# Conv-and-attention block on one NeuronCore: order of norm, third pooling level and low parts at the seam of two images

## The chip, the cores and the metric

The kernel runs on one core of a Trainium2 chip. The metric is the device time of one execution in microseconds; lower is better. All times in this text are microseconds unless marked ns. Engines: TensorE (PE in the profile; PEld is its weight load), VectorE (DVE), ScalarE (ACT), GpSimd (POOL), SyncE (SP).

## The reference

The input x is (8, 256, 32, 32), float32. Two blocks are applied, each on a group-normalised input and added to its own input:

```python
x = x + L0(_gn(x), ...)     # pooling and gated convolution
x = x + L1(_gn(x), w1, w2)  # attention over the 1024 pixels of an image

def L0(x):
    x_aux = silu(conv1x1(x, w_sta) + b)             # 256 -> 128 channels
    y1, y2 = [x_aux], [x_aux]
    for _ in range(3):
        y1.append(0.9 * maxpool5x5(y1[-1]) + 0.1 * sumpool5x5(y1[-1]) / 25)
        y2.append(sumpool5x5(e * y2[-1]) / (sumpool5x5(e) + 1e-6))   # e = exp(y - max)
    y = concat([silu(cv1(concat(y1))), silu(cv2(concat(y2)))])       # 512 channels
    a = y, through four depthwise convolutions of 3 taps (1x3, 3x1, dilated 1x3, dilated 3x1)
    a = conv1x1(a, w_c1)
    return silu(cvend(y * a))

def L1(x):   # per image, f: 1024 x 256
    q = f @ w1.T;  attn = softmax(q @ f.T / 16);  v = f @ w2.T
    return attn @ v
```

`_gn` normalises each image over groups of 8 channels: mean and variance over 8 channels and all pixels.

## The kernel before

All products are made of float32 matmuls whose operands are split in a high and a low part (each tile has a `_hi` and a `_lo`): three matmuls, hi x hi, lo x hi and hi x lo, stand for one. ScalarE makes the high parts (a copy), VectorE the low ones (value minus high part).

Phases A and B (up to about 270) normalise the input, make x_aux of all images, and the y2 levels of all images in HBM. Phase C is a loop over images, written as `step(i, conv, attn, chained, ahead)` on every engine, with an order of its own per engine, written out by hand. Step i does the convolution part of image i (`conv`), the attention part of image i - 1 (`attn`), and the pooling chain of image i + 1 (`chained`). Step 0 has no attention, steps 1 to 7 are full steps (both parts; in step 7 nothing is chained), step 8 has the attention of image 7 alone. Engines meet by counting semaphores.

TensorE in a full step: cv2(0), cv2(1) with a small matmul for the group means inside, then one for the group variances, cv1(0), cv1(1), q and v of the attention, then eight tiles of scores, transposes and products with v, then c1 (four) and cvend (two). A `product_split` of the convolution is 12 uses of a weight tile, each two matmuls of 512 columns. cv1(0) takes the low part of level 1 at use 7, that of level 2 at use 8, the high part of level 3 at use 9 and its low part at use 11. PSUM has three slots that rotate: product n can start when the reader of product n - 3 is done. The slot of the first v product (`("qv", 2)`) is that of the fourth cv product, which ScalarE's `silu_cv(3)` frees.

The pooling chain of an image: three levels (`middle` twice, `last`), each 5x5 maxima by VectorE (`maxima`, steps 0 to 6, the last one on `work_b`), 5x5 sums by accumulating DMAs that POOL issues one after another (`add_round`, eight rounds a level), and a mixture of both by VectorE (`mixture_of_added`, a wait on `columns_added`). `level_split_hi` and `level_split_lo` make the parts of a level for cv1. POOL's queue at a step's seam: last round of level 3, wait for its landing, the two first DMA issues of the next image's level 1 (L226, L228), the power for the norm (L1195), and then the accumulations of that level.

The norm of the attention input (image i - 1): VectorE `bn_stats` and `bn_aggr` at the end of step i - 1, TensorE `means` over channel groups, VectorE three small operations (dev, its square, spread), TensorE `variances`, VectorE two small operations (eps, negated mean), POOL the power -0.5, VectorE `shift`; ScalarE then makes the normalised image and its high part in two tiles, VectorE the low parts (`normalised_lo`), which q's product wants behind its first four matmuls.

The depthwise taps: ScalarE does the centre tap of a piece (`centre_tap(n)`), VectorE the two outer ones (`outer_taps(n)`); a centre tap waits for the outer taps of the piece's stage before.

## Time and profile before

| | us |
|---|---|
| median of three runs | 1384.13 |
| lowest, highest | 1377.48, 1387.42 |
| the profiled execution | 1376.88 |
| its span, first to last instruction | 1375.1 |
| busy in the span: TensorE, VectorE, ScalarE, POOL | 1206.2, 1152.7, 726.0, 293.6 |
| mean granted TensorE clock | 0.96 of full |

The profile is that of one execution. Around its span lie 1.8. Busy time of matmuls is modelled, as they are pipelined. In a timeline row, what stands in brackets is the idle time of the engine before that row and what ended it. A transfer's row is its issue alone.

### The profile page before, as it was taken

The page shows a single profiled execution, that of the slowest core. Times are in us where ns is not written, and L with a number is a line of the kernel's source. Part 1 is how long each engine was busy: PE and PEld are TensorE (multiplying, and loading weights), DVE is VectorE, ACT ScalarE, POOL GpSimd, SP SyncE. Part 2 cuts the span into 40 slices and gives each one's busy share as a digit, 9 for nine tenths or more (in the row PEclk, how much of TensorE's full clock was granted, in tenths as well). Part 3 has the DMA queues.
Part 4 walks back from the last instruction along what each step waited for, and adds up shares of the span by engine and source line. Part 5 has one row for each costly group of instructions (what it writes and reads, how often), then busy time and mean ns, then how long its engine had stood idle before and what let it go on. Part 6 is the DMA issues. An engine that isn't in the chain of part 4 may idle for free.

```text
span 1375.1 us, 17821 instructions
## 1 busy us (share of the span) xinstructions
PE 1206.2 (88%) x6730; PEld 1026.1 (75%) x6730; DVE 1152.7 (84%) x1220; ACT 726.0 (53%) x781; POOL 293.6 (21%) x247
## 2 busy tenths in 40 slices
PE   3559898766899999999899999999998999999697
PEld 1249898655678877877788788878887887797597
DVE  7779887799989889989998999899989977985343
ACT  0246667663375447536753675366546643853342
POOL 1566767401111111111111111111111111000000
PEclk9769999987999999999999999999999999999899
DMA  7403123253665566566456644764475466001000
GB/s 287 168 31 93 77 86 115 97 126 90 142 143 118 151 177 122 113 169 160 107 121 197 141 109 108 208 140 104 116 200 126 108 144 157 0 1 62 0 0 31
DMA packets 72303, 159.91 MB, mean 116 GB/s; under 512 B 33088, under 2 KB 35904, under 8 KB 72256
## 3 DMA queue, kind: packets, MB, share of 16 engines
q0 software_dynamic: 23904, 92.11, 29.9%
q1 hardware_dynamic: 47648, 66.85, 14.7%
q8 instruction: 32, 0.52, 0.2%
q10 hardware_dynamic: 704, 0.30, 0.1%
q14 instruction: 15, 0.12, 0.0%
HBM read 41.46 MB, written 25.17 MB: 48 GB/s over the span
## 4 chain that ended last, share of the span: by engine, by line
PE 36%; DVE 18%; issue 17%; ACT 6%; DMA 3%; DVEq 0%; POOL 0%; ACTq 0%; POOLq 0%
PE slot L1299 12%; PE slot L1246 10%; PE ps_level L1299 10%; DVE between L1574 4%; PE slot L1315 3%; DVE a L1574 2%; DMA boxes<-twos 2%; DVE pt_all L345 1%; ACT a L1478 1%; ACT between L1428 1%; DVE f_all L410 1%; DVE x L1617 1%; ACT f_all L1447 1%; ACT a L1428 1%; DVE tall L323 1%
## 5 line engine op out<-in xcount | busy, mean ns | idle before, releaser
L1299 PE MATMUL ps_level<-v_all,pt_all 128*128 128x256 f32 x1536 | 200.1, 287 | 13.6 <-DVE pt_all L1578 8.2
L1299 PEld LDWEIGHTS ps_level<-v_all,pt_all 128*128 128x128 f32 x1536 | 189.6, 192 | 17.3 <-DVE pt_all L1578 15.8
L1299 PE MATMUL slot<-f_all,q_all 128*128 128x512 f32 x768 | 189.7, 397 | 0.0
L1574 DVE SCALAR_TENSOR_TENSOR a<-between,k_columns,a 128x992 f32<-128x992 f32 (+1 forms) x128 | 157.6, 1232 | 6.9 <-ACT a L1428 4.6
L1299 PEld LDWEIGHTS slot<-f_all,q_all 128*128 128x128 f32 x768 | 140.1, 188 | 27.9
L1578 DVE TENSOR_TENSOR pt_all<-slot,pt_all 128x1024 fp32r<-128x1024 f32 x64 | 78.2, 1221 | 40.8 <-ACT pt_all L1442 40.6
L1451 ACT CAST v_all<-y 128x1024 fp32r<-128x1024 f32 x32 | 33.8, 1055 | 134.6 <-DVE y L1607 134.4
L1456 ACT ACTIVATE mixed<-ps_level,row_inv 128x256 f32<-128x256 f32 x64 | 30.2, 473 | 133.5 <-PE ps_level L1299 133.5
L1428 ACT ACTIVATE a<-between,k_columns 128x1024 f32<-128x1024 f32 x64 | 79.3, 1240 | 33.3 <-DVE between L1574 32.3
L1607 DVE SCALAR_TENSOR_TENSOR y<-slot,k_columns,y 128x1024 f32<-128x1024 f32 x32 | 40.9, 1282 | 57.0 <-PE slot L1246 55.1
L1574 DVE SCALAR_TENSOR_TENSOR between<-y,k_columns,between 128x992 f32<-128x992 f32 x64 | 78.8, 1249 | 7.8 <-ACT between L1428 6.6
L1442 ACT CAST pt_all<-slot 128x1024 fp32r<-128x1024 f32 x64 | 65.1, 1017 | 36.2 <-PE slot L1315 35.3
L1583 DVE TENSOR_REDUCE c_minus_max<-slot 128x1 f32<-128x1024 f32 x64 | 78.0, 1219 | 7.0 <-PE slot L1299 7.0
L1437 ACT ACTIVATE pooled<-slot,c_minus_max 128x1024 f32<-128x1024 f32 x64 | 71.6, 1118 | 21.8 <-DVE c_minus_max L1583 21.8
L1315 PE MATMUL slot<-k_ident,pooled 128*128 128x128 f32 x512 | 67.2, 274 | 15.9 <-ACT pooled L1437 15.9
L1574 DVE SCALAR_TENSOR_TENSOR between<-a,k_columns,between 128x960 f32<-128x960 f32 x64 | 77.2, 1215 | 1.1
L1315 PEld LDWEIGHTS slot<-k_ident,pooled 128*128 128x128 f32 x512 | 56.8, 141 | 19.9 <-ACT pooled L1437 19.9
L873 POOL TENSOR_TENSOR e_lo<-x_all,e_hi 128x1024 fp32r<-128x1024 f32 x24 | 61.3, 2552 | 43.4 <-ACT e_hi L828 43.4
L1246 PE MATMUL slot<-f_all,k_c_hi 128*128 128x512 f32 x232 | 64.7, 401 | 0.4 <-DVE y L1607 0.4
L1246 PE MATMUL slot<-f_all,k_c_lo 128*128 128x512 f32 x232 | 63.5, 396 | 0.0
L1246 PE MATMUL slot<-q_all,k_c_hi 128*128 128x512 f32 x232 | 63.5, 395 | 0.0
L1246 PE MATMUL slot<-q_all,k_cv_hi 128*128 128x512 f32 x192 | 59.4, 412 | 2.2 <-ACT q_all L405 2.2
(204 smaller groups left out, 2752.1 us busy)
## 6 DMA issues: line engine op xcount, KB each, us to landing
levels<-x_all SPq DMA_DIRECT2D x32, 512.0 KB, 2.6
boxes<-twos POOLq DMA_DIRECT2D x28, 543.0 KB, 4.8
boxes<-twos POOLq DMA_DIRECT2D x28, 527.0 KB, 4.6
x_all<-in_x SPq DMA_DIRECT2D x8, 1024.0 KB, 12.8
f_all<-levels SPq DMA_DIRECT2D x8, 1024.0 KB, 7.4
x<-in_x SPq DMA_DIRECT2D x8, 1024.0 KB, 5.9
out<-x SPq DMA_DIRECT2D x8, 1024.0 KB, 4.1
twos<-boxes POOLq DMA_DIRECT2D x14, 561.0 KB, 3.0
```

Of the source, the lines that this page charges most:

```text
L873: nc.gpsimd.tensor_tensor(e_lo[:, u], e[u], e_hi[:, u].bitcast(F32), ALU.subtract).then_inc(e_lo_done, 1)
L1246: last = nc.tensor.matmul(slot[:, hs], weights[:, k], inputs(k)[:, hs], start=(at == 0), stop=(at == len(uses) - 1))
L1299: last = nc.tensor.matmul(out, lhs, rhs, start=(n == 0), stop=(n == len(parts) - 1))
L1315: last = nc.tensor.transpose(slot[:, cols(m)], prob[:, cols(m)], keep["ident"][:, :])
L1428: nc.scalar.activation(dst, src, ACT.Identity, scale=keep["taps"][:, s, c, 1:2], bias=keep["b_taps"][:, s, c:c + 1]).then_inc(taps_centre. ...
L1437: nc.scalar.activation(prob[:, :], slots_of["s", t][:, :], ACT.Exp, bias=minus_max[:, t:t + 1], accum_out=row_sum[:, t:t + 1]).then_inc(pr ...
L1442: nc.scalar.copy(pt_hi[:, t % 2], slots_of["t", t][:, :]).then_inc(pt_hi_done.sem, 1)
L1451: nc.scalar.copy(y_hi[:, m], y[:, m]).then_inc(y_hi_done.sem, 1)
L1574: nc.vector.scalar_tensor_tensor(o, u, keep["taps"][:, s, c, tap:tap + 1], o, ALU.mult, ALU.add).then_inc(taps.sem, 1)
L1578: nc.vector.tensor_tensor(pt_lo[:, t % 2], slots_of["t", t][:, :], pt_hi[:, t % 2].bitcast(F32), ALU.subtract).then_inc(pt_lo_done.sem, 1)
L1583: nc.vector.tensor_reduce(minus_max[:, t:t + 1], slots_of["s", t][:, :], AX, ALU.max, negate=True).then_inc(maxed.sem, 1)
L1607: nc.vector.scalar_tensor_tensor(y[:, m], slots_of["c1", m][:, :], keep["b_c1"][:, m:m + 1], y[:, m], ALU.add, ALU.mult).then_inc(gated.se ...
```

## The change

It concerns the seam between two steps. On VectorE the three small operations of the norm come right behind maximum step 5 of level 3's maxima (step 6 follows them), eps and negated mean behind that; the third mixture then, low part 1 behind it, shift, low parts 2 and 3. Before, the order was maxima 5 and 6, low parts 1 and 2, small operations, mixture, eps and negated mean, low part 3, shift. The two low parts of the normalised image stand together, with both tap pairs behind them. At the end of step 0 the maxima 3 to 6 of level 3 leave their place between the sums of the two halves of the image and go behind the aggregation. On TensorE the variances' matmul goes from behind cv2(1) to behind its use 9. On ScalarE `silu_cv(1)` and the high part of level 3 change places.

```diff
@@ -1229,7 +1229,7 @@
                 def cols(m):
                     return slice(m * P, (m + 1) * P)
 
-                def product_split(kind, m, name, hi, lo, sig, order, hi_ready, lo_ready, between=None):
+                def product_split(kind, m, name, hi, lo, sig, order, hi_ready, lo_ready, between={}):
 
 
                     slot = claim(kind, m)
@@ -1245,8 +1245,8 @@
                             hs = slice(h * HALF, (h + 1) * HALF)
                             last = nc.tensor.matmul(slot[:, hs], weights[:, k], inputs(k)[:, hs],
                                                     start=(at == 0), stop=(at == len(uses) - 1))
-                        if between and at == len(uses) // 2:
-                            between()
+                        if at in between:
+                            between[at]()
                     last.then_inc(sig.sem, 1)
 
                 def tiles_of(t):
@@ -1255,7 +1255,7 @@
                 def when(sig):
                     return lambda n: wait(pe, sig, i, n + 1)
 
-                def cv2(m, between=None):
+                def cv2(m, between={}):
                     product_split("cv", m, "cv2", pooled.hi, pooled.lo, cv, pooled.ORDER, when(pooled.hi_done),
                                   when(pooled.lo_done), between)
 
@@ -1359,10 +1359,9 @@
                     cv2(0)
                     if not attn:
                         box_first()
-                    cv2(1, between=means if attn else None)
+                    cv2(1, between={6: means, 9: variances} if attn else {})
                 elif attn:
                     means()
-                if attn:
                     variances()
                 if conv:
                     cv1(0)
@@ -1468,8 +1467,8 @@
                             inputs_hi(c - 1)
                 elif conv:
                     silu_cv(0)
+                    silu_cv(1)
                     chain.level_split_hi(act, i, LEVELS)
-                    silu_cv(1)
                     for n in range(CT):
                         centre_tap(n)
                 if attn:
@@ -1632,8 +1631,6 @@
 
                 slots_of = slot_plan(conv, attn)
                 before = iter(range(BEFORE if attn else KT * STAGES))
-                if conv and attn:
-                    chain.level_split_lo(dve, i, LEVELS - 1)
                 if attn:
                     small = Steps(dve, norm, i - 1)
                     wait(dve, group_mean, i - 1, 1)
@@ -1645,7 +1642,7 @@
                 if chained and not attn:
                     chain.maxima(dve, i + 1, 0, first=chain.inner_ahead())
                 if conv and attn:
-                    chain.mixture_of_added(dve, i, LEVELS - 1)
+                    chain.maxima(dve, i, LEVELS - 1, MIX - 2)
                 elif conv:
                     outer_taps(next(before))
                     chain.mixture_of_first(dve, image2d(ps_level[:, :]))
@@ -1654,10 +1651,14 @@
                     small.did(nc.vector.tensor_scalar(spread[:, :], ps_ot[:, 0:CT], 1e-5, None, ALU.add))
                     small.did(nc.vector.tensor_scalar(gmean[:, :], ps_o[:, 0:CT], -1.0, None, ALU.mult))
                     if conv:
-                        chain.level_split_lo(dve, i, LEVELS)
+                        chain.mixture_of_added(dve, i, LEVELS - 1)
+                        chain.level_split_lo(dve, i, 1)
                     small.wait()
                     wait(dve, rstd_done, i - 1, 1)
                     small.did(nc.vector.tensor_tensor(shift[:, :], gmean[:, :], rstd[:, :], ALU.mult))
+                    if conv:
+                        chain.level_split_lo(dve, i, LEVELS - 1)
+                        chain.level_split_lo(dve, i, LEVELS)
                 if conv:
                     outer_taps(next(before))
                 if conv and attn:
@@ -1665,7 +1666,8 @@
                 if attn:
                     for t in range(CT):
                         normalised_lo(t)
-                        if conv:
+                    if conv:
+                        for t in range(CT):
                             outer_taps(next(before))
                 if conv:
                     for n in before:
@@ -1739,7 +1741,6 @@
                     wait(dve, chain.first_max, i + 2, MIX - 1)
                     level_maxima(2, 0, 1, 2)
                     add_l0(0)
-                    level_maxima(2, 3, 4, 5, 6)
                 else:
                     if ahead:
                         ahead_maxima(0, 1, 2)
@@ -1780,9 +1781,9 @@
                     for m in range(CT):
                         nc.vector.bn_aggr(mv[:, m, :], stats[:, m].rearrange("p h s -> p (h s)")).then_inc(bn.sem, 1)
                 if chained:
-                    if attn:
-                        level_maxima(2, 5, 6)
-                    chain.level_split_lo(dve, i + 1, 1)
+                    if not attn:
+                        level_maxima(2, 3, 4)
+                    level_maxima(2, 5)
 
             for n in range(KT):
                 pooled.split_lo(dve, 0, n)
```

## Rows read from the trace of the kernel before

**Rows 1.** Windows from one step's means to the next; x: instructions.

```profile
core 0: us, PE busy (x) PEld busy (x) DVE busy (x) ACT busy (x) POOL busy (x), PEclk, DMA share, GB/s
...
507.35:638.33 130.98, 123.05 (x686) 104.87 (x685) 119.86 (x128) 73.37 (x81) 19.89 (x26) 1.00 0.60 143
638.33:769.93 131.60, 124.23 (x685) 105.99 (x684) 119.94 (x128) 73.60 (x81) 19.93 (x26) 0.99 0.59 141
```

**Rows 2.** TensorE's timeline: start us, us, what, [idle before it, releaser].

```profile
850.45 1.09 PE L1315 MATMUL slot<-k_ident,pooled 128*128 128x128 f32 x8 [1.99 <-ACT pooled L1437]
...
900.92 0.28 PE L1335 MATMUL ps_level<-c_mv,k_group 128*128 128x2 f32 x2
...
904.67 0.38 PE L1335 MATMUL ps_level<-c_spread,k_group 128*128 128x2 f32 x2 [1.03 <-DVE c_spread L1644]
...
919.61 1.27 PE L1299 MATMUL slot<-f_all,k_w_hi 128*128 128x512 f32 x4 [2.33 <-DVE f_all L1603]
...
931.52 5.62 PE L1299 MATMUL slot<-f_all,q_all 128*128 128x512 f32 x24
...
948.93 3.14 PE L1299 MATMUL ps_level<-v_all,pt_all 128*128 128x256 f32 x24 [1.36 <-DVE pt_all L1578]
```

**Rows 3.** VectorE's timeline of step 5.

```profile
899.26 0.28 DVE L1781 BATCH_NORM_AGGREGATE c_mv<-c_stats 128x2 f32<-128x12 f32 x2 [0.16 <-DVE c_stats L1620]
899.46 1.17 DVE L323 TENSOR_TENSOR work_b<-work_a 128x1024 f32<-128x1024 f32 x1
...
904.66 1.22 DVE L332 SCALAR_TENSOR_TENSOR last<-boxes,work_b 128x1024 f32<-128x1024 f32 x1
...
907.00 1.23 DVE L345 TENSOR_TENSOR pt_all<-last,v_all 128x1024 fp32r<-128x1024 f32 x1 [0.85 <-ACT v_all L341]
...
909.14 4.99 DVE L1574 SCALAR_TENSOR_TENSOR between<-y,k_columns,between 128x992 f32<-128x992 f32 x4 [0.85 <-ACT between L1428]
...
915.88 2.54 DVE L1574 SCALAR_TENSOR_TENSOR a<-between,k_columns,a 128x992 f32<-128x992 f32 x2 [0.61 <-ACT a L1428]
...
921.92 4.85 DVE L1574 SCALAR_TENSOR_TENSOR between<-a,k_columns,between 128x960 f32<-128x960 f32 x4
...
926.69 2.35 DVE L1690 SCALAR_TENSOR_TENSOR q_all<-slot,q_all 128x1024 fp32r<-128x1024 f32 x2
...
932.77 1.23 DVE L1693 TENSOR_TENSOR v_all<-slot,v_all 128x1024 fp32r<-128x1024 f32 x1 [0.22 <-ACT v_all L1496]
...
934.46 1.23 DVE L1583 TENSOR_REDUCE c_minus_max<-slot 128x1 f32<-128x1024 f32 x1 [0.47 <-PE slot L1299]
```

**Rows 4.** VectorE's timeline of step 8, the first small operation.

```profile
1289.66 0.16 DVE L1640 TENSOR_TENSOR c_dev<-c_mv,ps_level 128x2 f32<-128x2 f32 x1 [0.60 <-PE ps_level L1335]
```

**Rows 5.** ScalarE's timeline of step 5.

```profile
905.92 1.05 ACT L341 CAST v_all<-last 128x1024 fp32r<-128x1024 f32 x1 [6.94 <-DVE last L332]
...
923.19 1.10 ACT L1421 ACTIVATE y<-slot,k_columns 128x1024 f32<-128x1024 f32 x1
```

**Rows 6.** POOL's timeline of step 2 and of step 5.

```profile
509.68 0.56 POOL L226 DMA_DIRECT2D twos<-ahead  x1 [4.82 <-issue]
...
902.38 0.56 POOL L226 DMA_DIRECT2D twos<-ahead  x1 [4.71 <-DMA boxes<-twos]
...
906.16 0.71 POOL L1195 TENSOR_TENSOR c_rstd<-c_spread,k_minus_half 128x2 f32<-128x2 f32 x1 [2.69 <-DVE gmean L1655]
```

**Rows 7.** Windows of 5 us behind two TensorE waits, columns as in rows 1.

```profile
657.00:662.00 5.00, 4.99 (x15) 3.96 (x16) 4.93 (x5) 2.51 (x4) 0.43 (x1) 0.66 0.58 111
...
850.00:855.00 5.00, 3.97 (x32) 3.77 (x32) 4.96 (x7) 3.82 (x7) 0.00 (x0) 1.00 0.68 172
```

**Rows 8.** The mixture's line in phase B: durations in ns, first and last start.

```profile
L332 DVE SCALAR_TENSOR_TENSOR last<-last,work_b x1: 3223/3223/3223, 226.2 to 226.2; 128x1024 f32<-128x1024 f32 x1
```

**Rows 9.** The timeline of step 1, TensorE and VectorE.

```profile
375.49 0.58 PE L1335 MATMUL ps_level<-c_mv,k_group 128*128 128x2 f32 x2 [5.99 <-DVE c_mv L1781]
...
380.12 1.23 DVE L332 SCALAR_TENSOR_TENSOR last<-boxes,work_b 128x1024 f32<-128x1024 f32 x1 [2.00 <-DMA boxes<-twos]
```

## The prediction

> **What bounds the kernel now.** First the windows cut at the matmul of the group means, one per full step [rows 1]: a step takes 131 us, TensorE is busy for 123 to 124 and VectorE for 120 of them, so neither hides the other, and what ends last has to be read place by place. Steps 2 to 7 of the seven full steps (images 1 to 7) repeat one pattern; step 5, from 900.92, is the one I follow. TensorE's timeline there [rows 2] shows three waits in front of the attention loop: 1.03 for c_spread, 2.33 for the second low part of the normalised image, 1.36 for a low part of the turned probabilities. The first two look like the change's prize. VectorE's timeline [rows 3] is to be read second: from the aggregation at 899.26 to the row maximum at 934.46 it idles in small pieces only: 0.85 (low part of level 3, for ScalarE's cast), 0.85 (first tap, ScalarE), 0.61 (third tap pair, ScalarE), and 0.47 before the maximum. At the maximum it waits for TensorE, but soon after TensorE waits 1.36 for VectorE [rows 2]. So VectorE's order bounds this stretch, TensorE's two waits are mostly slack, and the gain is what VectorE gains at the row maximum. Behind 948.93 the pattern is rigid, with both engines in step; an advance there is carried to the next aggregation.
>
> **Part by part, steps 2 to 7, in the clock of step 5.** A use of two 512-column matmuls is 0.47 (24 matmuls in 5.62, [rows 2]); large VectorE operations start 1.14 apart where nothing holds them (two take 2.35) and 1.25 where one needs the other's result (a full 1.22 and a little) [rows 3].
>
> *Small operations and variances moved forward.* The aggregation and maximum step 5 stay, until 900.63. The first small operation needs the means (900.92); in step 8, with nothing beside it, VectorE gets them 0.60 after its aggregation, matmul included [rows 4], so it starts at about 901.45, a new idle of 0.8. Three small operations end at 902.0. TensorE's place for the variances, behind use 9, comes at 900.92 + 0.14 + 3 x 0.47 = 902.46: no wait, and the second product ends at 903.8 instead of 903.6; the first product of cv1 starts at 903.8 instead of 904.9. Maximum step 6 fills VectorE from 901.97, eps and gmean follow at 903.15.
>
> *Third mixture, low parts.* The mixture runs at 903.3 (before: 904.66), low part 1 at 904.56, shift at 905.75, low parts 2 and 3 at 905.85 and 907.0. Before, ScalarE's cast had waited 6.94 for the mixture with everything queued behind it [rows 5]. Now silu_cv(1) (1.1) stands in front of the cast and runs from 904.0, the cast runs 904.9 to 905.9, and the two centre taps end before VectorE wants them: both pieces of 0.85 go. The power on POOL (0.71, [rows 6]) ends by 904.2; it queues behind the next image's two DMA issues, to 903.5, and POOL's next accumulation comes no later than before. TensorE wants low part 1 at use 7 (907.1), 2 at use 8 (907.5), 3 at use 11 (908.9); they end at 905.8, 907.0, 908.2. No wait, margins 0.5 and more. VectorE's first tap: 908.1 instead of 909.14, gain 1.0.
>
> *Both normalised low parts together.* ScalarE runs 2.0 ahead of its old times, so they run at 913.0 and 914.2 and end at 915.4; TensorE wants them at 903.8 + 24 x 0.47 + 0.9 = 916.0. The 2.33 goes. The 0.61 before the third tap pair goes too (its centre tap had been waiting behind nothing but ScalarE's queue): tap pair 4 starts at 920.2 instead of 921.92, the q low part at 925.0 instead of 926.69, gain 1.7.
>
> *What is late next.* TensorE finishes q at 920.6 and needs a slot that silu_cv(3) frees. That stands on ScalarE behind centre tap 5, and that behind VectorE's tap pair 3, which ends at 920.3: silu_cv(3) ends at 922.5 (before: 923.19 + 1.10 [rows 5]). So a new wait of 1.9, then 0.7 for the q low part. The first scores end at 931.8, just when VectorE is free (925.0 + 2.3 for q's low parts, 2.4 for a tap pair, 2.3 for v's low parts, whose 0.22 wait before the second goes [rows 3]): the row maximum at 932.0. Against 934.46 that is 2.4. Step 5 is one of three slow steps, though: its 2.33 wait was followed by a granted clock of 0.66 of full, the 1.2 GHz level for part of it; such a step is 131.60 long against 130.98 [rows 1, 7]. Against the steps at full clock the gain is 1.8.
>
> *Clock.* Sum without slow steps: 3 x 2.4 + 3 x 1.8 = 12.6. After the wait of 1.99 at the end of the attention loop the windows show 1.00 [rows 2, 7], and my new wait is 1.9, so I count one slow step in six. Its price: a clock of 0.66 over 5 us loses 1.7 of matmul time, of which the 0.7 and a little more lie under the wait for the q low part, which then falls away: about 0.9 is left. So 12.6 - 0.9 = 11.7; at worst six times 0.9 = 5.4 off.
> By the Trainium skill (TensorE: Matmul & The Clock Gate, What's actually happening) the gate is released by activity and the throttled state is the default, its monitor running free of the kernel's start; by that, fewer and shorter waits can only help on average, but which step is hit is chance, as the alternation of slow and full steps here suggests.
>
> *POOL beside VectorE.* Before, every power ran while VectorE idled or had just started a small tail (906.16, beside the 0.85 idle [rows 3, 6]); now it runs beside the mixture. The nearest row is far: the mixture that ran beside 1024-element POOL work took 3.22 against 1.22 [rows 3, 8]. For 2 elements I take 0; the other end is the power's whole 0.7 per step, 4.2 in all.
> The Trainium skill speaks against the change here (GPSIMD Engine Reference, Specifications): GpSimd shares its SBUF interfaces with VectorE and contends with VectorE instructions that have two SBUF inputs, as the mixture has; the trace agrees for large operands [rows 8], and by that rule the sum would be 8 instead of 12.
>
> *Step 1.* The two last-image sums come earlier there, since four maximum operations move behind them: TensorE's 5.99 wait for the aggregation [rows 9] shrinks to 1.2, but a wait of 2.7 for the spread and 3.3 for low part 1 follow, because the column sums land only at 380.1, where VectorE waits 2.00 already. From that mixture on, VectorE has 1.25 + 1.14 + 0.1 + 2 x 1.14 = 4.8 to its first tap instead of 4.48 (as in step 5, 904.66 to 909.14, idle included), and saves the 0.6: gain 0.3. Step 8 is not changed. In all 11.7 + 0.3 = **12.0 us**.
>
> **The rivals.**
> (A) *The column sums become the wait.* The mixture is wanted 1.4 earlier, at means + 2.4. POOL saw the sums at means + 1.46 in step 5 and + 2.33 in step 2 [rows 1, 2, 6]: margins 0.9 and 0.1. Where they land 1.5 or more later, each step does what step 1 does, 0.3: 7 x 0.3 = 2.1, 1382. For: step 1, thin margins, medians 7 above the profiled run. Against: the profile's own times. Chance 0.15.
> (B) *TensorE was the bound.* Then both waits count in full, and the slow clock of three steps: 6 x (1.03 + 2.33) + 3 x 0.6 = 22, 1362. Against: VectorE's queue, as above. Chance 0.09.
> (C) *Contention with POOL in full*: 12.0 - 4.2 = 8, 1376. Chance 0.12.
> (D) *Slower: late sums plus the clock.* If sums land later than means + 5 (use 7 of cv1's first product is passed by then), TensorE stops inside that product and again for silu_cv(3), runs at 1.2 GHz into the scores, and loses the 1.7 of row 7 against 0.3 gained: 6 x 1.4 = 8 slower, 1392. Place: level_lo_done in cv1(0). Chance 0.04.
> (E) *The variances stall the product anyway*, if the spread comes after 902.46 (margin 0.5). That is TensorE's slack and costs nothing until it exceeds what VectorE bounds; inside the forecast.
>
> **How the numbers follow.** The profiled execution took 1376.88 (span 1375.1), at the low end of the three runs (1377.48 to 1387.42); its rows give 1376.88 - 12.0 = 1364.9. On the median, 1384.13 - 12.0 = **1372**, 0.9% less. Chance 0.60 for this case, own range 1366 to 1377 (no slow step: 12.9 less; all slow: 7.5 less). The range 1362 to 1383 reaches to (C), (A) and (B), and takes in some 3 us of either median. One per cent, about what a measurement of this kernel can tell from no change, is 1370.3: below it lie (B) and some four tenths of the forecast, 0.35; above 1398 only the tail of (D), 0.03.
>
> **What would show it.** Right: no wait for c_spread inside the product, variances about 1.5 after the means; low parts of the normalised image back to back with no TensorE wait; a new TensorE wait near 1.9 for y (silu_cv(3)) before v's product; the row maximum 32.7 behind the aggregation (now 35.2); steps of 129 us. Wrong: VectorE idle at the mixture for columns (A), a mixture over 1.3 us (C), the first tap pair not earlier than aggregation + 9.5, or a full-step period that shrinks by 3 or more (B).

## The result and the profile after

The changed kernel takes 1368.84 (median of 8 runs, 1363.71 to 1373.67) against 1382.41 of the kernel before (8 runs, 1377.33 to 1387.45). The ratio is 0.9897, 95% interval 0.9871 to 0.9923: 1.0% faster, 14 us. Forecast: 1372, 0.9% and 12 us. The profiled execution took 1367.99, its span is 1366.2.

The windows cut at the group means again, steps 2 to 5 (these answer to [rows 1]):

```profile
core 0: us, PE busy (x) PEld busy (x) DVE busy (x) ACT busy (x) POOL busy (x), PEclk, DMA share, GB/s
...
509.07:638.06 128.99, 122.72 (x686) 104.99 (x685) 119.56 (x127) 73.46 (x81) 20.93 (x26) 1.00 0.60 144
638.06:768.56 130.50, 124.23 (x686) 106.54 (x684) 119.63 (x127) 73.27 (x81) 20.66 (x26) 0.99 0.57 139
768.56:901.11 132.55, 125.82 (x685) 107.92 (x684) 119.92 (x127) 73.42 (x81) 20.38 (x26) 0.97 0.59 141
901.11:1031.12 130.01, 123.00 (x685) 104.93 (x684) 119.75 (x127) 73.48 (x81) 20.43 (x26) 1.00 0.61 145
```

Steps of 129.0, 130.5, 132.6 and 130.0 stand where there were 131.0 and 131.6. They are not alike any more, and two things make them differ: late column sums and the granted clock. VectorE's timeline of step 5 shows the first, as [rows 3]. The aggregation is its row L1782, the row maximum its first row L1582 (the first maximum over a tile of scores):

```profile
899.44 0.28 DVE L1782 BATCH_NORM_AGGREGATE c_mv<-c_stats 128x2 f32<-128x12 f32 x2 [0.16 <-DVE c_stats L1619]
...
901.43 0.16 DVE L1637 TENSOR_TENSOR c_dev<-c_mv,ps_level 128x2 f32<-128x2 f32 x1 [0.62 <-PE ps_level L1335]
...
903.45 1.23 DVE L332 SCALAR_TENSOR_TENSOR last<-boxes,work_b 128x1024 f32<-128x1024 f32 x1 [0.17 <-DMA boxes<-twos]
...
906.71 0.16 DVE L1658 TENSOR_TENSOR c_shift<-gmean,c_rstd 128x2 f32<-128x2 f32 x1 [0.68 <-POOL c_rstd L1195]
...
909.10 4.99 DVE L1573 SCALAR_TENSOR_TENSOR between<-y,k_columns,between 128x992 f32<-128x992 f32 x4
914.00 2.35 DVE L1602 TENSOR_TENSOR f_all<-a,f_all 128x1024 fp32r<-128x1024 f32 x2
...
921.17 4.85 DVE L1573 SCALAR_TENSOR_TENSOR between<-a,k_columns,between 128x960 f32<-128x960 f32 x4
925.94 2.35 DVE L1692 SCALAR_TENSOR_TENSOR q_all<-slot,q_all 128x1024 fp32r<-128x1024 f32 x2
...
933.09 1.22 DVE L1582 TENSOR_REDUCE c_minus_max<-slot 128x1 f32<-128x1024 f32 x1 [0.16 <-PE slot L1299]
```

The three idle pieces of ScalarE's making (0.85, 0.85, 0.61) are gone; from the shift on VectorE doesn't wait until the row maximum. In their place stand 0.62 for the means, 0.17 for the column sums and 0.68 for the power. The first tap starts 9.66 behind the aggregation, little earlier than the 9.88 of before; in step 2, where sums and power were in time, it is 8.67. The row maximum comes 33.65 behind the aggregation here, 32.66 in step 2; before it was 34.6 or 35.2.

TensorE in step 5, as [rows 2]:

```profile
901.11 0.28 PE L1335 MATMUL ps_level<-c_mv,k_group 128*128 128x2 f32 x2
...
902.73 0.28 PE L1335 MATMUL ps_level<-c_spread,k_group 128*128 128x2 f32 x2
...
908.10 0.74 PE L1246 MATMUL slot<-pt_all,k_cv_hi 128*128 128x512 f32 x2 [0.32 <-DVE pt_all L345]
...
923.58 0.74 PE L1299 MATMUL slot<-k_w_hi,f_all 128*128 128x256 f32 x4 [2.14 <-ACT y L1420]
...
927.21 0.74 PE L1299 MATMUL slot<-k_w_hi,f_all 128*128 128x256 f32 x4 [0.55 <-DVE q_all L1692]
...
930.12 5.65 PE L1299 MATMUL slot<-f_all,q_all 128*128 128x512 f32 x24
...
947.55 2.66 PE L1299 MATMUL ps_level<-v_all,pt_all 128*128 128x256 f32 x20 [1.36 <-DVE pt_all L1577]
```

The wait for c_spread is gone, the variances come 1.62 behind the means; the wait of 2.33 for the normalised low part is gone. There is a new one of 2.14 for y, then 0.55 for the low part of q, and 0.32 for a level's low part. The 1.36 at the end is the same: VectorE's queue again.

ScalarE, as [rows 5], and POOL, as [rows 6]:

```profile
904.09 1.12 ACT L1420 ACTIVATE y<-slot,k_columns 128x1024 f32<-128x1024 f32 x1 [4.92 <-PE slot L1246]
905.10 1.04 ACT L341 CAST v_all<-last 128x1024 fp32r<-128x1024 f32 x1
...
922.44 1.09 ACT L1420 ACTIVATE y<-slot,k_columns 128x1024 f32<-128x1024 f32 x1
```

```profile
904.27 0.55 POOL L226 DMA_DIRECT2D twos<-ahead  x1 [4.70 <-DMA boxes<-twos]
904.81 0.55 POOL L228 DMA_DIRECT2D ahead_boxes<-ahead  x1
905.37 1.24 POOL L1195 TENSOR_TENSOR c_rstd<-c_spread,k_minus_half 128x2 f32<-128x2 f32 x1
```

The cast no longer waits, silu_cv(3) starts 23.0 behind the aggregation instead of 23.9. The power takes 1.24 instead of 0.71.

The end of step 3's attention loop, TensorE's timeline and then windows of 5 us behind that wait in steps 3, 4 and 5:

```profile
716.57 1.64 PE L1315 MATMUL slot<-k_ident,pooled 128*128 128x128 f32 x8 [1.99 <-ACT pooled L1436]
```

```profile
717.00:722.00 5.00, 5.00 (x31) 4.88 (x28) 4.96 (x7) 2.91 (x3) 0.00 (x0) 0.66 0.43 134
848.00:853.00 5.00, 3.86 (x22) 3.86 (x23) 4.95 (x6) 3.80 (x5) 0.00 (x0) 0.71 0.77 186
979.00:984.00 5.00, 3.31 (x28) 3.31 (x29) 4.51 (x7) 3.82 (x6) 0.00 (x0) 1.00 0.77 169
```

The wait of 1.99 is the same as before; the granted clock is 0.66 and 0.71 of full in steps 3 and 4 (partly at the 1.2 GHz level) and 1.00 in step 5. The windows of steps 4 and 5 begin 1.1 and 1.7 ahead of the wait's end (849.14 and 980.69); over the 5 us from its end on, steps 3 and 4 have 0.66 each. In the profile before no full step had this [rows 7], but step 8 did: 0.66 from 1359.71 to 1364.71.

With that, each step can be split in two: from the aggregation to the row maximum, and from there to the next aggregation. Worked out from the starts of these two rows in each step of the profiled execution of each kernel (step 7's second part is shorter, since nothing is chained there, and left out; step 1, which starts differently, is told where it matters):

| kernel | aggregation to row maximum, steps 2 to 7 | row maximum to next aggregation, steps 2 to 6 |
|---|---|---|
| before | 34.6 35.2 34.6 35.2 34.5 35.1 | 96.4 96.4 96.4 96.4 96.4 |
| changed | 32.7 32.6 34.7 33.7 32.5 32.5 | 96.4 97.9 97.9 96.4 96.4 |
| e1 pair only | 33.9 33.9 33.9 33.9 33.8 33.8 | 96.4 97.9 96.4 96.4 97.9 |
| e2 no pair | 32.7 32.6 32.6 32.6 32.5 32.5 | 96.4 97.9 96.4 97.9 96.4 |
| e3 variances behind | 33.6 34.3 34.3 34.3 34.2 33.0 | 96.4 96.4 97.9 96.4 98.4 |
| e4 ScalarE's order | 32.6 34.2 32.6 32.6 32.5 32.5 | 98.0 97.9 97.9 96.4 97.9 |
| e5 silu early | 32.7 35.0 35.6 32.6 32.5 32.7 | 97.9 98.6 96.4 98.0 96.4 |
| e6 power first | 32.6 32.6 32.6 32.6 32.5 32.5 | 97.1 97.4 97.2 97.2 98.0 |
| e7 short sums, changed | 32.7 32.6 32.6 32.6 32.5 32.5 | 97.9 96.4 97.9 96.4 97.9 |
| e8 short sums, before | 34.6 34.6 35.2 35.3 35.1 35.1 | 97.9 96.4 98.0 97.9 97.9 |
| e9 filled wait, before | 34.6 35.2 34.6 35.2 34.5 34.5 | 96.4 96.4 96.4 96.4 96.4 |
| e10 filled wait, changed | 34.1 32.6 32.6 32.6 34.7 32.5 | 96.4 96.4 96.4 96.4 96.4 |
| e11 no idle | 32.0 32.0 32.8 32.0 31.9 31.8 | 96.4 97.9 98.1 96.4 97.9 |
| e12 no idle, filled | 33.5 32.0 32.0 32.0 33.8 31.8 | 96.4 96.4 96.4 96.7 96.4 |

The first column takes few values: one that the order of work sets, about 0.65 more where the clock is lower behind a wait, 1 to 3 more where the sums or the power are late. The second is mostly 96.4 or 1.5 more; e6 has a value of its own.

The record also has each run's mean granted clock. Its median is 0.952 over 70 runs of the kernel before (those beside e1 to e12) and 0.960 over the 8 runs of the changed kernel. Within the kernel before time goes with it: the 7 runs above 0.957 have a median of 1377.5, the 14 up to 0.948 one of 1386.2. The two profiled executions stand at 0.960 and 0.961, and they differ by 8.9, not 14. So some 5 us of the 14 go with the clock (an estimate from these numbers; which causes which they don't show).

### The profile page after: what moved, and what is told of

Same layout as the page of the kernel before. It is cut to its first block, busy times and chain, and to the rows that moved or that the text cites. A ratio compares the mean times of both kernels' runs of the same rounds, so it can differ in the third digit from the quotient of the medians.

```text
span 1366.2 us, 17821 instructions
## 1 busy us (share of the span) xinstructions
PE 1203.1 (88%) x6730; PEld 1027.2 (75%) x6730; DVE 1148.9 (84%) x1220; ACT 725.3 (53%) x781; POOL 297.5 (22%) x247
## 4 chain that ended last, share of the span: by engine, by line
PE 30%; DMA 19%; issue 16%; DVE 12%; ACT 2%; POOL 1%; POOLq 0%; DVEq 0%; ACTq 0%
PE slot L1299 10%; PE ps_level L1299 10%; DMA boxes<-twos 8%; PE slot L1246 6%; DMA twos<-boxes 4%; DVE between L1573 4%; PE slot L1315 3%; DMA ahead_boxes<-twos 3%; DVE a L1573 3%; DMA twos<-middle 2%; DMA twos<-ahead 1%; DMA twos<-ahead_boxes 1%; DVE middle L332 1%; DVE pt_all L345 1%; DVE pt_all L1577 1%
## 5 line engine op out<-in xcount | busy, mean ns | idle before, releaser
L1450 ACT CAST v_all<-y 128x1024 fp32r<-128x1024 f32 x32 | 33.7, 1055 | 136.6 <-DVE y L1606 136.4
L1427 ACT ACTIVATE a<-between,k_columns 128x1024 f32<-128x1024 f32 x64 | 79.4, 1240 | 32.6 <-DVE between L1573 31.6
L1582 DVE TENSOR_REDUCE c_minus_max<-slot 128x1 f32<-128x1024 f32 x64 | 78.0, 1219 | 6.3 <-PE slot L1299 6.2
L1420 ACT ACTIVATE y<-slot,k_columns 128x1024 f32<-128x1024 f32 x32 | 35.4, 1106 | 56.9 <-PE slot L1246 56.9
```

The source lines that it names most:

```text
L1420: nc.scalar.activation(y[:, c], slots_of["cv", k][:, :], ACT.Silu, bias=bias).then_inc(y_ready.sem, 1)
L1427: nc.scalar.activation(dst, src, ACT.Identity, scale=keep["taps"][:, s, c, 1:2], bias=keep["b_taps"][:, s, c:c + 1]).then_inc(taps_centre. ...
L1582: nc.vector.tensor_reduce(minus_max[:, t:t + 1], slots_of["s", t][:, :], AX, ALU.max, negate=True).then_inc(maxed.sem, 1)
```

## The experiments

Theory Q says that VectorE's queue sets the gain, rival T that TensorE's two waits did.

**e1, pair only.** The kernel before, with

```diff
                     for t in range(CT):
                         normalised_lo(t)
-                        if conv:
-                            outer_taps(next(before))
+                    if conv:
+                        for t in range(CT):
+                            outer_taps(next(before))
```

> The kernel before, with one part of the change alone: the two low parts of the normalised image one behind the other, both tap pairs behind them. Theory Q (VectorE's queue sets the gain): only the idle of 0.6 before the third tap pair goes, 0.6 x 7 = 4 us, ratio to before 0.997; TensorE's wait of 2.3 for the second low part goes, and a wait of about 1.7 for y before v's product takes its place; row maximum 34.0 to 34.6 behind the aggregation. Rival T (TensorE's waits bound it): the 2.3 counts in full, 16 us, ratio 0.988.

Measured 1371.59, ratio 0.9912 (0.9883 to 0.9941). The time is nearer to T's than to Q's. The profile (step 3; VectorE, then TensorE) is Q's to the tenth:

```profile
637.23 0.28 DVE L1782 BATCH_NORM_AGGREGATE c_mv<-c_stats 128x2 f32<-128x12 f32 x2 [0.16 <-DVE c_stats L1620]
...
652.04 2.35 DVE L1603 TENSOR_TENSOR f_all<-a,f_all 128x1024 fp32r<-128x1024 f32 x2
...
671.13 1.23 DVE L1583 TENSOR_REDUCE c_minus_max<-slot 128x1 f32<-128x1024 f32 x1 [0.15 <-PE slot L1299]
```

```profile
661.63 0.74 PE L1299 MATMUL slot<-k_w_hi,f_all 128*128 128x256 f32 x4 [1.69 <-ACT y L1421]
```

The row maximum is 33.90 behind the aggregation, 0.7 less than the 34.6 of a step at full clock and 1.35 less than the 35.2 of the others; all six steps are alike, since the 2.33 wait, and the lower clock behind it, is gone. That makes 6 x 0.7 + 3 x 0.65 = 6.2 in the rows. The profiled run took 1373.95, with two steps at 97.9, against 1376.88 with none: the rows account for 3 of it, and the medians are 12 apart. So a usual execution of the kernel before is slower than the one profiled, for something that the row maximum doesn't show. The clock goes with it: its median is 0.952 in the 24 runs of the kernel before and 0.9585 in the 8 of e1. Beyond the lower clock behind the 2.33 wait, where that comes from isn't shown; it isn't the wait that e9 fills, which e1 leaves as it was, with the lower clock behind it in two of the five steps of the table.

**e2, no pair.** The changed kernel with the same lines put back.

> The changed kernel, with the two low parts interleaved with tap pairs again. Theory Q: VectorE has the same work and no idle, since the centre tap it needs is ready by then; TensorE gets its wait of about 2.2 for the second low part back and loses the one of 1.6 to 2.1 for y in its place; time as the changed kernel, ratio to before 0.990. Rival T: 2.2 x 7 = 15 us come back, ratio 1.000.

Measured 1365.71, ratio 0.9865 (0.9828 to 0.9903): nothing comes back. Step 3, VectorE and TensorE:

```profile
636.74 0.28 DVE L1781 BATCH_NORM_AGGREGATE c_mv<-c_stats 128x2 f32<-128x12 f32 x2 [0.16 <-DVE c_stats L1619]
...
669.35 1.22 DVE L1582 TENSOR_REDUCE c_minus_max<-slot 128x1 f32<-128x1024 f32 x1
```

```profile
655.14 1.20 PE L1299 MATMUL slot<-f_all,k_w_hi 128*128 128x512 f32 x4 [1.66 <-DVE f_all L1602]
...
663.50 0.74 PE L1299 MATMUL slot<-k_w_hi,f_all 128*128 128x256 f32 x4 [0.55 <-DVE q_all L1691]
```

The wait for the second low part is there again (1.66, expected 2.2), that for y (1.72) is gone, the row maximum stays at 32.61. The wait has only moved, so this test says less against T than expected, but nothing of T's 15 us came back, and within the whole change the pair contributes nothing. e5 tests T once more. Alone (e1) it removed VectorE's 0.61; in the changed kernel ScalarE is early enough without it.

**e3, variances behind.** The changed kernel with

```diff
-                    cv2(1, between={6: means, 9: variances} if attn else {})
+                    cv2(1, between={6: means} if attn else {})
                 elif attn:
                     means()
+                if attn:
                     variances()
```

> The changed kernel, with the variances' matmul behind the second product again, VectorE's order as changed. Theory Q: VectorE, which wants the variances 3.6 behind the aggregation, gets them at 4.7; each full step loses 1.0 to 1.2 there, less where the column sums are late anyway: 6 to 7 us of the gain go, ratio to before 0.995, VectorE idle of about 1 before the eps operation. Rival T: TensorE has the same work, at most a wait of 0.5 for level 3's low part: 0 to 3 us, ratio 0.990 to 0.992.

Measured 1376.27, ratio 0.9942 (0.9919 to 0.9965). VectorE, step 2:

```profile
511.65 0.28 DVE L1783 BATCH_NORM_AGGREGATE c_mv<-c_stats 128x2 f32<-128x12 f32 x2
...
516.21 0.16 DVE L1652 TENSOR_SCALAR c_spread<-ps_level 128x2 f32<-128x2 f32 x1 [0.83 <-PE ps_level L1335]
...
516.41 1.23 DVE L332 SCALAR_TENSOR_TENSOR last<-boxes,work_b 128x1024 f32<-128x1024 f32 x1
...
545.23 1.23 DVE L1583 TENSOR_REDUCE c_minus_max<-slot 128x1 f32<-128x1024 f32 x1
```

VectorE idles 0.83 for the variances, the mixture is 0.94 later, the row maximum 33.58 instead of 32.66; TensorE's wait for y grows to 2.14 in every step, and in four of six steps the lower clock follows (34.2 to 34.3). By the ratios that is 6 us, nearly half of the gain, for a matmul that comes two uses later.

**e4, ScalarE's order.** The changed kernel with `chain.level_split_hi(act, i, LEVELS)` ahead of `silu_cv(1)` again.

> The changed kernel, with the high part of level 3 ahead of silu_cv(1) on ScalarE again. Theory Q: since the mixture comes 1.4 earlier, the cast runs from 4.8 behind the mixture's new place and ScalarE is only 0.6 later than changed; the centre tap is still ready 0.2 before VectorE wants it: time as the changed kernel, ratio 0.990, no idle of VectorE before the first tap. Rival S (ScalarE's swap is what removed the two idle pieces of 0.85): 1.7 x 6 = 10 us come back, ratio 0.997.

Measured 1370.82, ratio 0.9930 (0.9898 to 0.9962): the interval holds 0.990, not 0.997. The row maximum is 32.6 in five steps, as changed; in step 3 it is 34.2, where VectorE waits 0.68 for the power and the clock behind a wait of 2.15 for y is 0.66. Rival S is out: not the swap removed the two pieces of 0.85, but the mixture's earlier place.

**e5, silu early.** The changed kernel with

```diff
-                    for n in range(3, BEFORE - 2):
+                    for n in range(3, BEFORE - 3):
                         centre_tap(n)
                     silu_cv(3)
-                    centre_tap(BEFORE - 2)
+                    for n in range(BEFORE - 3, BEFORE - 1):
+                        centre_tap(n)
```

> The changed kernel, with silu_cv(3) on ScalarE one centre tap earlier (before centre tap 5 in place of behind it), so that TensorE gets its slot for v's product sooner. Theory Q: TensorE's wait of 1.6 to 2.1 for y shrinks to about 0.5, but the next thing it needs, q's low part, is VectorE's: the wait for q grows from 0.55, the row maximum moves by 0 to 0.3; 0 to 2 us less than the changed kernel, ratio to before 0.988 to 0.990. Rival T: 1.6 x 7 = 11 us less, ratio 0.982.

Measured 1376.68, ratio 0.9954 (0.9922 to 0.9985): slower than the changed kernel by half a per cent, where both theories had it equal or faster. TensorE's timeline in step 2:

```profile
534.01 0.73 PE L1299 MATMUL slot<-k_w_hi,f_all 128*128 128x256 f32 x4 [2.54 <-DVE q_all L1693]
```

The wait for y is gone and that for q is 2.54: two waits (1.72 and 0.56) have become one, a little longer than both. The row maximum is 32.65, as Q says: T, which wanted 1.6 a step, is out. In steps 3 and 4, where the power was late (0.68 each, in step 4 with sums 1.27 late as well), that wait is 2.99 and 2.98, the clock behind it is lower, and the maximum 35.0 and 35.6, over 34.7, the latest of the changed kernel. In the second column three of five steps are over 97; the lower clock stands there behind the unchanged wait of 1.99. It isn't the long wait as such: behind those of 2.54, 2.54, 2.42 and 2.59 in steps 2, 5, 6 and 7 the clock is 1.00. The median clock of the twelve runs is 0.953 (changed kernel 0.960), so the loss goes with the clock, but why this order has it more often stays open.

**e6, power first.** The changed kernel with, on POOL,

```diff
                 if chained:
                     if attn:
-                        chain.add_level(pool, i + 1, 0, first=1)
+                        chain.waited(pool, chain.columns_added, i, 48 * LEVELS)
+                        chain.add_level(pool, i + 1, 0)
                     chain.add_level(pool, i + 1, 1)
                     chain.add_level(pool, i + 1, 2)
-                if ahead:
-                    chain.waited(pool, chain.columns_added, i + 1, 48 * LEVELS)
-                    chain.add_level(pool, i + 2, 0, end=1)
```

> The changed kernel, with the norm's power first in POOL's queue of a step and the wait for the column sums and the next image's two DMA issues behind it. In the profile of the changed kernel VectorE idles 0.68 for the power in steps 1, 4 and 5, where the sums landed late and the power queued behind two issues of 0.55. Theory P (queueing on POOL costs that): the idle goes, 3 x 0.7 = 2 us, ratio to before 0.988; the power starts about 3.8 behind the aggregation in every step. Rival M (the power is slow since it runs beside VectorE, 1.05 to 1.74 against 0.71): it stays as slow, but ends by 5.6 in every step, before VectorE wants it at 6.2; the same time by both, so what tells them apart is its duration: over 1.0 by M, 0.7 if the two issues were what lengthened it.

Measured 1374.85, ratio 0.9939 (0.9908 to 0.9969). POOL and VectorE in step 2:

```profile
509.38 1.74 POOL L1195 TENSOR_TENSOR c_rstd<-c_spread,k_minus_half 128x2 f32<-128x2 f32 x1 [5.85 <-DVE gmean L1650]
511.09 0.60 POOL L226 DMA_DIRECT2D twos<-ahead  x1
```

```profile
550.84 1.23 DVE L332 SCALAR_TENSOR_TENSOR middle<-ahead_boxes,early 128x1024 f32<-128x1024 f32 x1 [0.67 <-DMA ahead_boxes<-twos]
```

The idle for the power is gone in all steps, step 1 too, and the row maximum is 32.5 to 32.6 in six of six. The power takes 1.74 with nothing in front of it: rival M holds for its duration. But the next image's first DMA issue now stands behind it, 5.6 behind the aggregation, and the first mixture of that image waits 0.63 to 0.88 for its sums in steps 2 to 5; there the second column is 0.7 to 0.9 higher (the 98.0 of step 6 is the lower clock behind the wait of 1.99). In the rows that takes back 3 us for the 2 won: a moved instruction moves what is queued behind it. The ratio is worse than that, 0.0042 or 6 us above the changed kernel's, while the profiled execution (1366.76, of runs from 1363.05 to 1381.52) is 1.2 faster than the changed kernel's; the rest of those 6 us isn't explained.

**e7 and e8, short sums.** The changed kernel and the kernel before with

```diff
+            end = 4 * PITCH if level == LEVELS - 1 else ROWS
-            pool.dma_start(boxes[:, PITCH:ROWS], twos[:, 2 * PITCH:PITCH + ROWS],
+            pool.dma_start(boxes[:, PITCH:end], twos[:, 2 * PITCH:PITCH + end],
```

> The changed kernel, with the last accumulating DMA of level 3's column sums cut to three rows (the sums of the other rows lack one term), so that it lands some 2 us earlier. Theory D (late column sums take part of the gain back): the waits of 0.2 to 4 for the sums at the mixture and of 0.68 for the power go or shrink: 2 to 4 us less than the changed kernel, ratio to before 0.987; the row maximum 32.5 behind the aggregation in all steps 2 to 7 at full clock. If the sums are not a bound in most executions: 0 to 1 us, ratio 0.990.

> The kernel before, with the same DMA cut to three rows. Theory D: before, the mixture was wanted 1.4 to 1.6 later, so only step 1 waits (2.0): 0 to 2 us less, ratio 0.999 to 1.000. If the sums were late in most executions of the kernel before: 5 us and more, ratio below 0.997.

e7: 1365.53, ratio 0.9879 (0.9844 to 0.9914); e8: 1383.70, ratio 1.0010 (0.9988 to 1.0032). With early sums the changed kernel's row maxima are 32.5 to 32.7 in all six steps and the mixture's waits in them are gone; that is worth 2.5 us by the ratios, less than the intervals are wide, and 3 us by the rows of the profiled execution (34.7 and 33.7 against 32.6). Before the change the sums bound nothing. So the change did bring the sums within reach of the mixture, as rival A says, but only in some steps, and the price is not clear of the noise.

**e9 and e10, the filled wait.** The kernel before and the changed kernel with matmuls whose result is written over:

```diff
-                    wait(pe, prob_done, i - 1, t + 1)
                     slot = claim("t", t)
+                    if t == TILES - 1:
+                        for n in range(7):
+                            nc.tensor.matmul(slot[:, 0:HALF], keep["c1_hi"][:, 0, 0:P], keep["c1_hi"][:, 0, :],
+                                             start=True, stop=True)
+                    wait(pe, prob_done, i - 1, t + 1)
```

> The kernel before, with seven 512-column matmuls, whose result is written over, put into TensorE's wait of 1.99 for the last probabilities of an image (end of the attention loop). In the profiles so far the time from the row maximum to the next aggregation is either 96.4 or 97.9 in a step; where it is 97.9 the granted clock behind that wait is 0.66. The profile of the kernel before has none of these, that of its copy with the short sum four. Theory C (the wait, and with it the lower clock, is what costs these 1.5): all steps at 96.4 to 96.5, and as a usual execution of the kernel before has some four such steps, 4 to 6 us less, ratio 0.996. Rival: it isn't the wait that lowers the clock; 97.9 still occurs, and the seven matmuls cost 0 to 2 us, ratio 1.000 to 1.001.

> The changed kernel with the same seven matmuls. Theory C: no step with 97.9; about 2 to 4 us less than the changed kernel, ratio to before 0.988. If the lower clock was what the change saved, and not VectorE's queue, this kernel and the filled kernel before would come out alike; by theory Q they differ by the 10 to 11 us of the row maxima (32.6 against 34.6).

e9: 1374.26, ratio 0.9960 (0.9945 to 0.9976). e10: 1363.78, ratio 0.9881 (0.9861 to 0.9902). TensorE in e9, end of step 3's loop:

```profile
717.97 1.87 PE L1315 MATMUL slot<-k_c_hi 128*128 128x512 f32 x7
720.21 1.09 PE L1319 MATMUL slot<-k_ident,pooled 128*128 128x128 f32 x8 [0.36 <-ACT pooled L1441]
```

The wait is 0.36 instead of 1.99, and no step of the table stands at 97.9 in either kernel. (e10's step 1 takes 98.6, with a lower clock behind a wait of 1.82 for pt_all.) In steps 1 to 7 of the eleven profiles without the filling, the clock behind the wait of 1.99 is lower 37 times in 77; in the three with it (e9, e10, e12) it is 1.00 all 24 times, step 8 included. Useless work makes the kernel before 0.4% faster: the lower clock behind that wait costs a usual execution 5.5 us (3.3 to 7.6 by the interval), which the profiled one happened not to pay but in step 8. Between the two filled kernels the ratios differ by 0.0079, 11 us, uncertain by some 3.5; the profiled executions differ by 7.4, their row maxima by 9.3 in all. That is the change with this one chance taken out, and it fits Q's 10 to 11. The lower clock behind the wait of 2.33 stays in e9 (steps 3 and 5) and is part of what the change saves.

**e11, no idle.** The changed kernel with VectorE's order at the seam once more changed: maximum step 6 in front of the small operations, low part 1 in its place behind them, low part 2 in front of the shift.

```diff
+                if conv and attn:
+                    chain.maxima(dve, i, LEVELS - 1, MIX - 2)
                 if attn:
                     small = Steps(dve, norm, i - 1)
...
                 if conv and attn:
-                    chain.maxima(dve, i, LEVELS - 1, MIX - 2)
+                    chain.level_split_lo(dve, i, 1)
...
                         chain.mixture_of_added(dve, i, LEVELS - 1)
-                        chain.level_split_lo(dve, i, 1)
+                        chain.level_split_lo(dve, i, LEVELS - 1)
...
                     if conv:
-                        chain.level_split_lo(dve, i, LEVELS - 1)
                         chain.level_split_lo(dve, i, LEVELS)
```

> The changed kernel with VectorE's remaining idle of 0.6 (for the means) filled: maximum step 6 ahead of the small operations, low part 1 behind them (in place of step 6), low part 2 ahead of the shift (so that the slow power on POOL has time). Theory Q: first tap pair 0.5 to 0.6 earlier, 8.1 behind the aggregation instead of 8.65, row maximum 32.1 instead of 32.6, and 0.6 to 1 less sensitive to late sums: 3 to 5 us less than the changed kernel, ratio to before 0.987. Rival T (TensorE): its variances come 0.6 later, up to 0.2 of wait: 0 to 1 us more, ratio 0.990.

Measured 1365.22, ratio 0.9905 (0.9877 to 0.9933). VectorE in step 2:

```profile
504.07 0.28 DVE L1783 BATCH_NORM_AGGREGATE c_mv<-c_stats 128x2 f32<-128x12 f32 x2
...
506.62 0.15 DVE L1639 TENSOR_TENSOR c_dev<-c_mv,ps_level 128x2 f32<-128x2 f32 x1
...
508.24 0.15 DVE L1653 TENSOR_SCALAR c_spread<-ps_level 128x2 f32<-128x2 f32 x1
...
508.38 1.22 DVE L332 SCALAR_TENSOR_TENSOR last<-boxes,work_b 128x1024 f32<-128x1024 f32 x1
...
510.86 0.15 DVE L1660 TENSOR_TENSOR c_shift<-gmean,c_rstd 128x2 f32<-128x2 f32 x1
...
512.06 4.98 DVE L1573 SCALAR_TENSOR_TENSOR between<-y,k_columns,between 128x992 f32<-128x992 f32 x4
...
536.03 1.22 DVE L1582 TENSOR_REDUCE c_minus_max<-slot 128x1 f32<-128x1024 f32 x1
```

No idle is left in this step; first tap 7.99 and row maximum 31.96 behind the aggregation, 0.1 better than expected. The profiled run took 1360.51, 7.5 less than the changed kernel's; but the ratio, forecast at 0.987, doesn't tell the two kernels apart (0.9905 and 0.9897).

**e12, both.**

> Both: VectorE's idle filled as in the one before, and the seven matmuls at the end of the attention loop. If the two add: 0.984 to 0.986 of before; row maximum 32.1 and 96.4 behind it in every step, a step of 128.5 us. If the clock falls elsewhere in its place (behind the wait for y, as where that wait alone was long), 0.988.

Measured 1360.07 (1358.51 to 1361.36), ratio 0.9859 (0.9839 to 0.9879): within what adding both gives, and the lowest ratio of all, though its interval overlaps with those of e2 and e10. The row maximum is 31.8 to 32.0 in four steps; in steps 2 and 6 it is 33.5 and 33.8, with the power late (0.68) and a clock of 0.66 behind waits of 1.87 and 2.16 for y. So the case expected second, a lower clock elsewhere, came in part too.

## Why the prediction was right

The time (1372 forecast, 1368.84 measured) and the likeliest case held, and VectorE's part by the steps named. That 12 and 14 lie so close is partly luck: the rows of the profiled executions give 8.9 where the forecast has 12.0, and the clock, forecast to cost 0.9, goes with some 5 us on the side of the gain.

- *VectorE's queue bounds the stretch.* Right: e1 and e2 remove and restore TensorE waits of 1.7 to 2.3 and e5 the one for y, and at full clock the row maximum moves only by VectorE's own idle; e3 changes VectorE's wait by 0.83 and the row maximum by 0.92, and e11 takes out the last idle of 0.62 and moves it by 0.7.
- *Small operations and variances.* dev at 2.0 behind the aggregation (forecast 2.2), a new idle of 0.62 (0.8), no TensorE wait, variances 1.62 behind the means (1.54).
- *Mixture and low parts.* First tap 8.67 where nothing was late (8.8). Both pieces of 0.85 went. e4 corrects the reason: the earlier mixture did it, ScalarE's swap wasn't needed.
- *Pair of low parts.* No wait, as forecast, but e2 shows that without the pair there is nothing lost either: the 0.61 before the third tap pair, counted in this part, goes by ScalarE's lead alone (in e1 it went by the pair alone).
- *What is late next.* y with 1.6 to 2.1 (1.9), then q with 0.55 (0.7), row maximum 32.5 to 32.7 (32.7).
- *The sum.* The row maxima of steps 2 to 7 gain 1.9 + 2.6 - 0.1 + 1.6 + 2.0 + 2.6 = 10.6; forecast 12.6 without the clock. In the four steps with nothing late the gain is 1.9 to 2.0 or 2.6, a little over the forecast's 1.8 and 2.4. Steps 4 and 5 fall short by 3.1 together: the column sums were late (idle 0.45 and 0.17) and the power behind them (0.68 each), 2.0 in all, rival A in part; the rest is mostly the lower clock behind step 4's wait for y. The margins of 0.9 and 0.1 were rightly called thin.
- *Clock.* The term with the wrong sign and size. Behind the new wait for y the clock was lower in one step of six (step 4), as counted. But the statement that a wait of 1.99 is followed by full clock rested on one execution, and on its full steps alone: in its step 8 the clock behind that wait was 0.66. e8 had the lower clock there in four of five steps, the changed kernel in two, at 1.5 each. It was an old cost and not one of the change: e9 prices it at 5.5 us before, and e10 against the changed kernel at 0.0016 of ratio, 2 us, both uncertain by some 2 to 3. Some 3 us of the 14 measured may come from this; that is as large as the uncertainty, and it isn't shown. By the clocks of all runs some 5 us go with the clock, the three lower clocks behind the 2.33 wait (0.65 each) among them; where the rest arises, stays open.
- *Step 1.* Wrong: forecast a gain of 0.3, measured a loss. From the mixture to the row maximum it is 29.64 against 29.16, because the power ended late (0.68); and the sums landed at 381.3 instead of 380.1. That landing varies: the third mixture of step 1 starts between 377.7 and 382.1 in the other profiles with the new order at the end of step 0 and full sums, and at 380.2 and 380.9 in e1 and e9, so one execution doesn't price it.
- *POOL beside VectorE (rival C).* The price was put on the wrong side. VectorE's mixture took 1.23 beside the power as it did alone; the power took 1.05 to 1.74 instead of 0.71. It cost nothing where it started in time (e6: 1.74 in steps 2 to 7, no wait) and was part of the wait of 0.68 where the sums were late. The Trainium skill (GPSIMD Engine Reference, Specifications) states the contention of GpSimd with VectorE instructions that have two SBUF inputs; these runs agree that there is one, and add that for this pair the one that slows is POOL.

The profiled executions differ by 8.9: 7.6 in steps 2 to 7 (10.6 less two times 1.5 behind the row maximum), 3.0 in step 8, whose code is the same (1.5 up to its first row maximum, 1.5 behind, where the clock after the wait of 1.99 was 0.66 before and 1.00 in the changed kernel), and minus 1.7 before step 2. The 14 of the ratio come from 16 runs and are the better number for the time; for what the order of work is worth by itself, e9 against e10 is the nearest.

## What to carry to other kernels

When two engines are both over 90% busy in a stretch, the longer wait is not the one that counts: ask for each engine whether it has idle time of its own up to the point where they meet next, and price a change by the idle that it takes out of the one that has none left over. One profiled execution of a kernel can be a lucky one: before pricing by its rows, compare its own time and mean granted clock with the medians of the runs, and look for the value that a repeated stretch doesn't take in it. And before moving an instruction forward in an in-order queue, look at what stands behind it: the power moved to the front of POOL's queue won 2 us in the rows and cost 3.

## What the runs showed of the hardware

- The granted clock over the 5 us behind a TensorE wait of 1.99 is 1.00 in some steps and 0.66 in others, in the same execution and with the same instructions; where it is lower, the step is 1.5 longer. Filling the wait to 0.36 removed it: lower 37 times in 77 without, never in 24 with it (e9, e10, e12).
- The length of a wait alone doesn't tell what follows. The 31 waits for y of 1.57 to 1.72 (steps 2 to 7 of the changed kernel, e1, e4, e6, e7 and e10) were all followed by 1.00; of the 14 of 2.13 to 2.16 (the same kernels, e3 and e12, step 1 included) 9 by 0.66 to 0.68; the four of 2.42 to 2.59 for q in e5 by 1.00.
- A POOL power of 2 elements a partition takes 0.70 to 0.71 where VectorE waits for it or for ScalarE (kernel before, steps 2 to 8) and up to 1.77 (e3) beside VectorE operations of 1024 elements, which take 1.21 to 1.23 either way.
- Useless matmuls in a wait made the kernel before faster, by 0.4% (ratio 0.9960, 0.9945 to 0.9976, e9).
